# A decoder block: the input's first batch moved to ScalarE's queue, and four constant products ahead of it

## What is computed

```
x = layernorm(x + attn(x, Wq, Wk, Wv, Wo))     # rank-64 scores, softmax, 4 batches of 256
x = layernorm(x + xattn(x, token_ids, ctx))    # one of 4 "experts" per token, by its id
x = layernorm(x + ffn(x, Wr, br, Wg, Wu, Wd))  # top-1 of 4 experts, 1024 wide, by a router
```

## Time and profile before

| | us |
|---|---|
| median of 3 runs | 210.68 |
| lowest, highest | 210.64, 213.09 |
| the profiled execution | 211.95 |
| its span | 210.2 |
| TensorE busy in it | 180.8 (86%) |
| VectorE, ScalarE, POOL busy | 131.8, 98.8, 112.6 |
| mean granted TensorE clock | 0.95 |

### The profile page before, as it was taken

The page is one execution under the profiler, slowest core; times in us unless marked ns, Lnnn a source line. Parts: engine busy times, 40 slices in busy tenths (PEclk is TensorE's granted clock), DMA queues, the critical chain, the costliest instruction groups (busy, mean ns, idle before and its releaser), DMA issues.

```text
span 210.2 us, 3907 instructions
## 1 busy us (share of the span) xinstructions
PE 180.8 (86%) x979; PEld 143.9 (68%) x979; DVE 131.8 (63%) x407; ACT 98.8 (47%) x254; POOL 112.6 (54%) x140
## 2 busy tenths in 40 slices
PE   1999988989691988589899999999999999999910
PEld 0877767656470875157688887888888888888710
DVE  4279977517742568765466537455489996888850
ACT  2157768044331462335566485664366632344530
POOL 6033467799003347674387506885068850266783
PEclk9999999799998599799999999999999999999985
DMA  5999921359999103134445430545304000011010
GB/s 159 347 363 420 364 78 56 116 158 303 342 338 408 51 26 108 31 89 107 111 154 161 153 138 0 154 150 168 134 2 153 0 0 3 0 42 62 20 58 22
DMA packets 15301, 29.14 MB, mean 139 GB/s; under 512 B 1710, under 2 KB 11952, under 8 KB 15154
## 3 DMA queue, kind: packets, MB, share of 16 engines
q1 hardware_dynamic: 13552, 25.68, 36.8%
q0 software_dynamic: 1440, 3.22, 4.3%
q10 hardware_dynamic: 290, 0.01, 0.1%
HBM read 20.41 MB, written 9.28 MB: 141 GB/s over the span
## 4 chain that ended last, share of the span: by engine, by line
PE 58%; POOL 12%; DMA 11%; issue 8%; DVE 5%; SPq 2%; ACT 1%; POOLq 1%; DVEq 0%; ACTq 0%
PE bank L464 13%; PE bank L466 12%; PE bank L465 12%; DMA x_sorted<-padrow 8%; POOL out_tokens L453 5%; PE bank L702 4%; PE bank L529 3%; POOL rstd L382 3%; PE bank L478 2%; PE bank L560 2%; PE bank L538 2%; DMA arena<-in_xT 2%; POOL rstd L414 2%; SPq L294 2%; POOL x_sorted L426 1%
## 5 line engine op out<-in xcount | busy, mean ns | idle before, releaser
L378 POOL TENSOR_TENSOR w_lo<-stage,w_hi 128x512 fp32r<-128x512 f32 x48 | 61.2, 1300 | 44.9 <-ACT w_hi L773 44.9
L864 ACT ACTIVATE gate<-bank 128x256 f32<-128x256 f32 x44 | 17.0, 387 | 48.5 <-PE bank L466 45.2
L1165 DVE TENSOR_TENSOR hid<-bank,gate 128x256 f32<-128x256 f32 x44 | 18.7, 424 | 30.5 <-ACT gate L864 30.2
L464 PE MATMUL bank<-w_hi,xr 128*128 x88 | 35.8, 407 | 1.9 <-DVE xr L1129 1.7
L466 PE MATMUL bank<-w_hi,xr 128*128 x88 | 34.8, 395 | 0.0
L465 PE MATMUL bank<-w_lo,xr 128*128 x88 | 34.7, 394 | 0.0
L464 PE MATMUL bank<-w_hi,hT 128*128 x88 | 28.5, 324 | 0.7 <-DVE hT L1170 0.7
L773 ACT ACTIVATE w_hi<-stage 128x512 fp32r<-128x512 f32 x48 | 28.6, 630 | 0.3 <-PE bank L466 0.3
L466 PE MATMUL bank<-w_hi,hT 128*128 x88 | 24.9, 283 | 0.0
L465 PE MATMUL bank<-w_lo,hT 128*128 x88 | 24.8, 282 | 0.0
L464 PEld LDWEIGHTS bank<-w_hi,xr 128*128 128x128 f32 x88 | 16.7, 189 | 4.9 <-issue 2.8
(11 more groups left out here) (176 smaller groups left out, 329.8 us busy)
## 6 DMA issues: line engine op xcount, KB each, us to landing
stage<-in_w_ffn SPq DMA_DIRECT2D x16, 768.0 KB, 4.7
x_sorted<-padrow SPq DMA_DIRECT2D x1, 4356.0 KB, 17.0
rows<-x_sorted SPq DMA_DIRECT2D x22, 132.0 KB, 2.2
buf<-in_x_tok SPq DMA_DIRECT2D x1, 1024.0 KB, 10.9
w_hi<-in_ctx SPq DMA_DIRECT2D x1, 1024.0 KB, 11.5
w_hi<-in_ctxT SPq DMA_DIRECT2D x1, 1024.0 KB, 14.0
x_sorted<-padrow SPq DMA_DIRECT2D x1, 792.0 KB, 12.6
arena<-in_xT SPq DMA_DIRECT2D x1, 768.0 KB, 6.7
```

What stands on the lines that cost most here:

```text
L378: g.tensor_tensor(out=lo, in0=src, in1=hi.bitcast(F32), op=ALU.subtract).then_inc(split_lo, 1)
L464: mm(dst, xhi, whi, start=start, stop=False)
L864: a(gate[:, (T + j) % 2, :], fA[j % 2][:, 0:FQ], ACT.Silu).then_inc(silu_done, 1)
L1165: v.tensor_tensor(out=hid[:, (T + j) % 2, :], in0=fA[j % 2][:, FQ:2 * FQ], in1=gate[:, (T + j) % 2, :], op=ALU.mult).then_inc(h_done, 1)
```

## The change

Three edits. The first batch of xT is started by ScalarE as its first transfer, ahead of ids, wr and br, and SyncE no longer starts it; the view of the source moves out of SyncE's function for that. POOL sets `ones` first among the constants, ahead of `padrow`. TensorE waits for one constant only, which is `ones`, and runs four constant products in place of two; the wait for all 22 constants that stands ahead of L498 is there already and stays.

```diff
@@ SyncE
-            xT_rows = xT_in.rearrange("p (k n) -> p k n", k=DK)
             sp.dma_start(awt[:, 0:QKW], aw[:, 0:QKW]).then_inc(d_aqk, 16)
-            sp.dma_start(xT[:, :, 0:SEQ], xT_rows[:, :, 0:SEQ]).then_inc(d_xT0, 16)
             sp.dma_start(awt[:, QKW:], aw[:, QKW:]).then_inc(d_avo, 16)
@@ POOL
+            const(g.memset(ones[:], 1.0))
             const(g.memset(padrow[:], 0.0))
             const(g.memset(ident[:], 1.0))
             const(g.memset(below[:], 1.0))
-            const(g.memset(ones[:], 1.0))
@@ TensorE
-            pe.wait_ge(consts, CONSTS)
-            idle_products(2)
+            pe.wait_ge(consts, 1)
+            idle_products(4)
             pe.wait_ge(d_aqk, 16)
             pe.wait_ge(d_xT0, 16)
             qk_of(0)
@@ ScalarE
+            act.dma_start(xT[:, :, 0:SEQ], xT_rows[:, :, 0:SEQ]).then_inc(d_xT0, 16)
             act.dma_start(ids[:], ids_in).then_inc(d_ids, 16)
```

More of the change, by code:

```diff
@@ L264, in route_kernel @@
         items = [(q, t) for q in range(NQ) for t in range(T)]
+        xT_rows = xT_in.rearrange("p (k n) -> p k n", k=DK)
         block = ctx.enter_context(nc.Block())
```

## The result

| | before | changed |
|---|---|---|
| median of 20 runs, us | 211.13 | 212.10 |
| ratio to before | | 1.0046, 95% interval 1.0026 to 1.0067 |
| the profiled execution's span | 210.2 | 210.6 |

The changed kernel is slower by 0.46 per cent, about 1.0 us. The others of either kernel still lie 3 us apart, so all that follows rests on ratios with their intervals and on where single steps lie in the profiles, not on single times.

What follows compares the result with a forecast made beforehand. The prediction took the chain through the end of the Wv Wo product (9.65) as the bound. An earlier start of qk_of(0) gave -0.22 and an unchanged clock rise 0, so 210.68 - 0.2 = 210.5 us, range 208.9 to 212.6.

Steps and rivals of the forecast that it cites:

- What bounds the kernel: Front of the kernel: what moves the Wv Wo product's end, 9.65, moves the kernel's end by as much, unless a transfer becomes late.
- the sum: End of Wv Wo: start of qk_of(0) 0.44 earlier counts half, -0.22; clock rise unchanged, 0; product ends at 9.43.
- The landing: First batch of xT: issued 0.44 earlier on ScalarE with its old duration, it lands at 4.73 instead of 5.16.
- The rival with the shared engines: Batch shares with Wv and Wo and lands at 5.94; product end +1.9 us, median 212.6; chance 0.27.
- The clock: TensorE during qk_of(0) and Wv Wo: clock still rises at 8.5, so this term adds 0.
- The end at r/2 + s/2 + 2.75: End of Wv Wo from s, the start of qk_of(0), and r, the clock's rise; half of what either moves counts.
- the lower bound r = 7.6: Earliest clock rise counted from a start at 4.86, after 2.7 us of work; Wv Wo would end at 9.0, -0.65.
- The start of before, 5.30: Start of qk_of(0) in the kernel before, taken as 0.14 behind the landing; forecast to move to 4.86.
- the cover: Slack ahead of L498: ids, starting at most 0.71 later, stay hidden by 2.8 us behind the Wv Wo product.
- The rival with the clock raised early: Early products raise the clock before the batch lands; Wv Wo ends at 8.1, -1.5 us, median 209.2; chance 0.18.
- the case I forecast: Whole kernel, likeliest case: median 210.5, from 210.0 to 211.2; chance 0.49.

Runs made afterwards that it cites:

- the kernel with ids first: The changed kernel with ten early products instead of four and ids ahead of the batch in ScalarE's queue; 0.9999 to the kernel before.
- the changed kernel's second: Profile of the changed kernel run again unaltered, as reference for other runs on that chip; 1.0055 to the kernel before.
- the one without products: The changed kernel with no constant products ahead of qk_of(0) instead of four; 1.0057 to the kernel before.
- run 32: Not a follow-up run: the words say that TensorE had run 32 small products (L518), from 35.72 to 39.46, in the kernel before; no ratio belongs to it.
- the ten-product kernel: The changed kernel with ten early constant products in place of four; 0.9982 and, on another chip, 0.9945 to the kernel before.
- the nine-product kernel: The kernel before with `ones` first and nine early products from 1.05, transfers untouched; 0.9961 and, on another chip, 0.9926 to the kernel before.

## Why the prediction was wrong

The prediction forecast a gain of 0.2 us, from two terms: the batch lands at 4.73, and the clock rises at 8.5 as before. Both failed; the kernel became 1.0 us slower.

**What bounds the kernel: right.** In twelve of the fourteen profiles the fill was issued 38.2 to 38.6 us behind the end of Wv Wo, for ends from 8.09 to 11.24. The front of the kernel is on the path, microsecond for microsecond, up to there. In the other two (40.5 and 40.8) the clock was still low through z_of(0), so that the late rise cost some 2 us more behind Wv Wo, which the sum, made for the end of Wv Wo, doesn't count.

**The landing: wrong.** I took the row's own duration, 3.92, with the earlier issue: 4.73. The changed kernel's profile shows 4.84 us, and the six profiles with the batch first in ScalarE's queue and Wv and Wo in SyncE's show 4.38 to 5.92, mean 5.1; the six with it in SyncE's show 4.4 to 5.16, mean 4.6. So by the means the move delays it by some 0.5 us, where I had -0.44; the two ranges overlap, and six against six don't settle the size. Two errors lie in it. The duration I started from, 3.92, was the longest of the six that SyncE's queue later showed (3.2 to 3.9): one profile was read as if it were the typical one. And I let "the faster start and the sharing pull opposite ways" stand for a cancellation that no row supported. The rival with the shared engines had the direction, and I gave it 0.27. Its 5.94, the batch done only when its neighbour is, was an assumption that no row of before showed; the changed kernel's profiles have the batch at 5.64 and 4.38, and Wv and Wo both times at 5.7. Its mechanism, a batch that loses to its neighbour in the other queue, is seen in the kernel with ids first; in the changed kernel only a rest of 0.03 MB moves beside Wv and Wo in one profile and none in the other, so there it is likely and not shown. Its sum has a slip: with a rise at 11.2 not all twelve records are done at 0.43 each (that takes to 11.55); the formula gives 11.4. In the means of the profiles the batch lost more than the 0.44 that its earlier issue had won.

**The clock: wrong, and the larger part in the changed kernel's profile** (1.11 of the 1.59). The end at r/2 + s/2 + 2.75 holds for the later profiles in which the clock rose within Wv Wo: for the changed kernel's second, s = 4.52 and r = 6.57 + 4.7 x 0.43 = 8.6 give 9.3 (9.29 measured); for the one without products, 6.05 and 10.5 give 11.0 (11.02). That is no test, as r is worked out from the same records. (Its paces, 0.43 and 0.216, are those of L620 and L529, and the r = 8.5 of before is 8.37 by the trace's own clock record.) The failed step is r itself. I kept r at 8.5 while writing that the early products no longer join up with qk_of(0), and that counted from 4.86 the rise lies at 7.6 to 10.0. The middle of that is 8.8, not 8.5, and with a start at 5.2 rather than 4.86 it is 9.1. My reading, which no run shows by itself: once the products are gone from in front of it, r is no longer fixed by products at 4.11 but hangs on the landing, so that a late batch is paid in full, not by half. That would be the interaction of the two edits: products alone 1.0000 and 0.9974, the transfer alone 1.0017, both 1.0046 and 1.0055. With the mean landings, s stays at about 5.2 (before: 5.14 to 5.30, the end of the two products or the landing; changed: 5.1 + 0.14), and r goes from 4.11 + 4.4 = 8.5 to 5.2 + 4.4 = 9.6, taking the 4.4 us between the start of the work and the rise from the first profile: the sum gives +0.55 us, 0.26 per cent. Measured were 0.46 (0.26 to 0.67) and 0.55 (0.20 to 0.91) per cent, so this carries about half of it. The 4.4 us may be too short: in the changed kernel's first profile the clock rose 6.0 us after qk_of(0) had started, and 6.2 after it with only the products moved, against 4.1 and 4.4 in the second profile and in the one without products. The three profiles of the changed kernel with four or no products end Wv Wo at 11.24, 9.29 and 11.02, on average 0.9 us or 0.4 per cent behind the 9.65 of before, which is about what was measured; but with 2 us between them, three profiles against one show it only roughly. Why the clock rises after 4 us in one execution and after 6 in another stays open.

One of the two rows that I took for rises elsewhere was misread. Their moments hold: beside the means of 0.75 and 0.89 the granted clock reads 0.50 in 41 to 42 and 72 to 73, and 1.00 in 43 to 44 and 74 to 75, so each mean is a stretch with both. The products at 39.81 don't follow an idle engine: TensorE had run 32 small products (L518) from 35.72 to 39.46, and only 0.33 us were empty. So the 2.7 us there are not counted from the start of work, and the lower bound r = 7.6 had no row behind it.

**The start of before, 5.30, misread.** I took it as set by the landing. In five of six profiles the batch in SyncE's queue landed by 4.64, ahead of 5.14, where the two products end; in the one I had, landing (5.16) and products (5.14) tied, and the chain named the landing. So with the products where they were, an earlier landing could win 0.16 us at most (5.14 against 5.30), not 0.44, and in most executions nothing; and with them moved, the start to compare with was nearer 5.14 than 5.30.

**The late ids: the cover was overstated.** I moved their landing by 0.71, to 3.8; it moved by 2.8, to 5.9. In all six profiles with 256 KB ahead of them in the queue the 4 KB landed after those, 0.2 to 1.5 us later, at 5.8 to 6.2. The cover of 2.8 us on L498 shrank to 0.7 in the changed kernel's second profile (counts at 8.61, Wv Wo at 9.29), and is gone in the ten-product kernel. In the changed kernel itself it cost nothing, so the step failed without moving the time.

**The rival with the clock raised early**: it doesn't occur with four products (the same ratio with none), and does with nine or ten: Wv Wo at 8.09, where the rival's sum gave 8.1. That the two numbers meet so closely is in part luck: qk_of(0) started 0.2 later than the rival had it and its first record, behind the products without a hole, was 0.3 shorter. Four and nine products, all else alike, end Wv Wo at 10.24 and 8.09.

**Chances and range.** The change lay within 2 per cent and the median, 212.1, within the range, but only because the range was drawn wide enough for the late rival (212.6). The sign was wrong: the case I forecast, from 210.0 to 211.2, did not come, and the one beside it did at less than its full price of 1.9.

## What to carry to other kernels

Work meant to raise TensorE's clock was worth something here only where it reached up to the work that it was for: fill the gap to the landing (nine products gave 0.9961, four 1.0000), and take the number from the latest landing seen: in one profile ten of them and a hole of 0.6 us, with the clock not yet risen, left it low for 4.3 us more. A hole of 0.68 did nothing in another, where it had. The version that follows, the kernel before with `ones` first and nine products from 1.05 on, is faster than both kernels: 0.9961 and 0.9926 to before, about 1.2 us. A transfer on the critical path that stands ahead of its rival in one queue had better stay there: a queue of its own started it 0.44 earlier and let the rival run beside it, it landed at 5.1 in the mean where it had landed at 4.6, in no comparison here was the moved transfer the faster one (1.0017 to 1; 0.9982 to 0.9961; 0.9945 to 0.9926), and the small table behind it landed after it, at 5.8 to 6.2 instead of 3.1. And a start time of one profile that two events share within 0.02 us has to be costed for both.

## What the hardware showed that was not expected

- The landing of one and the same transfer (256 KB, first in its queue at 0.80) varied from 4.38 to 5.92 over six executions, where in the queue of its rival it varied from 4.4 to 5.16. Issued at 1.25, 0.01 us after the rival in the other queue, it had moved almost nothing by 4.0 and landed at 5.97.
- A transfer of 4 KB issued behind 256 KB in one queue landed 4.3 to 4.7 us after its issue instead of 2.3 to 2.4, and 8.3 us after it with 768 KB ahead.
- After ten products without a hole, 4.45 us, and 0.6 us of nothing, the clock was still the low one (0.43 us a record) and stayed there for 4.3 us more. In another execution with ten products it rose at about 4.1, 3 us after the first of them, and 0.68 us of nothing left it up. In the nine-product kernel's first profile it rose within qk_of(0), some 4 us after the first product.
- The clock at one place differs between executions of a kernel: Wv Wo of the changed kernel took 3.41 us in one profile and 2.73 in the other.
